# A graph layer's last stage: 8 of the 17 row tiles of a chunk split into float32r heads and tails before they are summed

## The chip, the cores and the metric

The kernel runs on one core of one Trainium2 chip. The metric is the device time of one execution in microseconds (us), lower is better. The times shown are those of three runs; the profile is of one profiled execution.

## What is computed

Two graph layers over 3125 nodes with 512 features and 50000 edges that are sorted by their destination. The first is attention over the edges, the second (the one that the change touches) a mean over neighbours with two linear maps:

```python
deg = jnp.maximum(segment_sum(ones, dst, 3125), 1.0)
h = jnp.maximum(_layernorm(x), 0.0)
x = x + attention_layer(h, ...)
h = jnp.maximum(_layernorm(x), 0.0)
agg = segment_sum(h[src], dst, 3125)
x = x + h @ W1.T + b1 + (agg / deg[:, None]) @ W2.T + b2
```

## The kernel before

The nodes are cut into 25 windows of 125, and the edges, sorted by destination, into chunks of up to 17 tiles of 128 edges (`CT = 17`). With this input there are 25 chunks, one for each window. The program sorts the edges on VectorE, runs the attention layer chunk by chunk, then the output product and the second normalisation (which stores the rows of h in the table `h2tab` in HBM), and then the last stage, which is what matters here. It takes the last 600 us or so of the span, and goes through the 25 chunks so:

- **GpSimd** (POOL) only gathers. For each tile `gather` (L494 on, the instruction is L501) issues one indirect DMA that reads 128 edge numbers from `idx` in SBUF and fetches 128 rows of 512 float32 out of `h2tab` into `arena` (seen as `rows`, two buffers of 17 tiles). The 17 tiles come in four parts, `PARTS = [(0, 3), (3, 4), (7, 5), (12, 5)]` (first tile, count), each with its own semaphore `rows_in` for rows that have landed and `rows_free` for rows that PE has finished with. The next chunk is gathered while this one is summed.
- **TensorE** (PE) adds the rows up by destination: for each tile one float32 product of the one-hot matrix `oh` (128 edges by 125 nodes, stationary) with the 128 by 512 rows (L907) into `aggp` in PSUM. In front stands a small product for the degrees (L903), behind it the product of the window's own rows with W1 (`product`, L758), the transposes of the mean `win_out` and of the next window's rows (`fin_cols`, L893), and the product with W2 (L758 again).
- **VectorE** (DVE) scales and adds the sum (L1453 to L1459), decodes the edge words of the chunk after next (L1230 to L1237), makes its one-hot matrix (`one_hot`, L1246, both inputs in SBUF) and reduces that for the degrees (L1401), and last adds the bias and the old x of this chunk (L1470, L1473).
- **ScalarE** (ACT) copies the transposed columns out of PSUM (L705), twice a chunk.
- **SyncE** (SP) loads edge words and the window's rows, and stores the output; it waits for `out_ready` of a chunk before it goes on to the loads of the next.

All order is by the program text and semaphores: no scheduler moves an instruction.

## Time and profile before

| what | value |
| --- | --- |
| median of 3 runs | 1963.72 us (1957.36 to 1965.88) |
| profiled execution: span from the first to the last instruction | 1960.7 us |
| profiled execution: its own time, taken as its span and the 3 us by which the median lies above it | 1963.7 us |
| TensorE busy | 1657.7 us (85%) |
| VectorE busy | 1368.6 us (70%) |
| GpSimd busy | 1143.8 us (58%) |
| ScalarE busy | 989.2 us (50%) |
| last stage, from its first gather (at 1363.0 us) to the end | 597.7 us |

The span is what the profile measures; the time of an execution holds a little more. For the execution with the profile no time of its own is given, so the table sets its span beside the median. Busy shares are averages over stages that differ: in the last stage ScalarE has almost nothing to do and TensorE nearly no pause. Busy time of TensorE is modelled from pipelined instructions, so the starts of its instructions are a better measure than their durations. A float32 product shows as two matmul instructions for each call.

### The profile page before, as it was taken

Reading aid. Unit: us, or ns where it says so; the run is one execution under the profiler, and the core shown is the slowest. Engines: PE = TensorE matmul, PEld = TensorE weight load, DVE = VectorE, ACT = ScalarE, POOL = GpSimd, SP = SyncE. Lnnn points to the kernel's source line nnn. Section 1 sums busy time; section 2 is a strip of 40 time slices with the busy share of each in tenths; the row PEclk is TensorE's granted clock in tenths of the full one; section 3 lists DMA queues with packets and bytes.
Section 4 is the critical chain, followed back from the end, with each engine's and each line's share of the span. In section 5 each row is a group of like instructions: output and inputs, shape, how many; then the busy total and the mean of one; then the engine's idle time right before and its main releaser. Section 6 shows DMA issues by size and latency. Waiting matters only on the chain.

```text
span 1960.7 us, 24166 instructions
## 1 busy us (share of the span) xinstructions
PE 1657.7 (85%) x5685; PEld 957.1 (49%) x5685; DVE 1368.6 (70%) x2637; ACT 989.2 (50%) x3754; POOL 1143.8 (58%) x1322
## 2 busy tenths in 40 slices
PE   3799842198989898988888888886999999999998
PEld 1343321066666665666666666443444444444443
DVE  8889888588989898989898987367344444444441
ACT  4453310659999999999999998242000000000000
POOL 2000000477888788878787882012777777777773
PEclk9899876599999999989998988898999999999999
DMA  8122101655666666656565652864777777777774
GB/s 185 53 66 79 62 30 42 192 162 152 181 170 178 172 177 171 177 165 183 164 184 159 189 155 56 198 155 122 211 216 216 217 220 212 222 218 215 209 215 141
DMA packets 133203, 318.09 MB, mean 162 GB/s; under 512 B 41908, under 2 KB 42158, under 8 KB 133044
## 3 DMA queue, kind: packets, MB, share of 16 engines
q0 software_dynamic: 70240, 229.93, 41.2%
q1 hardware_dynamic: 62804, 86.44, 15.9%
q8 instruction: 50, 0.82, 0.2%
q14 instruction: 109, 0.89, 0.1%
HBM read 280.43 MB, written 35.86 MB: 161 GB/s over the span
## 4 chain that ended last, share of the span: by engine, by line
PE 59%; DVE 22%; issue 11%; DMA 3%; ACT 2%; DVEq 1%; POOL 1%; SPq 0%; POOLq 0%; ACTq 0%
PE sums L907 19%; PE wide L758 17%; PE sums L810 11%; PE wide L838 8%; DVE arena L1061 3%; DVE arena L1060 3%; DVE nodes L1352 2%; DMA h2tab<-node 2%; DVE nodes L1298 1%; DVE nodes L1343 1%; DVE node L1239 1%; ACT node L705 1%; PE wide L753 1%; ACT arena L579 1%; PE wide L771 1%
## 5 line engine op out<-in xcount | busy, mean ns | idle before, releaser
L625 ACT ACTIVATE nodes<-arena,nodes 128x64 f32<-128x64 f32 x2840 | 682.7, 332 | 1.7 <-PE sums L810 1.5
L501 POOL DMA_INDIRECT arena<-ktab,idx x425 | 425.2, 1001 | 174.7 <-issue 115.4
L501 POOL DMA_INDIRECT arena<-h2tab,idx x425 | 444.1, 1045 | 135.7 <-issue 133.5
L810 PE MATMUL sums<-nodes,oh 128*125 128x260 f32 x1768 | 465.3, 406 | 44.1 <-DVE nodes L1298 44.1
L758 PE MATMUL wide<-w_sb,node 128*125 128x512 f32 x1000 | 468.4, 612 | 22.6 <-ACT node L564 14.2
L810 PEld LDWEIGHTS sums<-nodes,oh 128*125 128x125 f32 x1768 | 340.4, 197 | 120.3 <-DVE nodes L1298 55.5
L907 PE MATMUL sums<-arena,oh 128*125 128x512 f32 x850 | 374.8, 599 | 6.6 <-DMA arena<-h2tab,idx 6.6
L838 PE MATMUL wide<-q_win,node 125*128 125x512 bf16 x1275 | 311.5, 382 | 5.4 <-issue 5.4
L705 ACT ACTIVATE node<-wide 128x500 f32<-128x500 f32 x51 | 27.2, 585 | 569.5 <-PE wide L893 569.5
L758 PEld LDWEIGHTS wide<-w_sb,node 128*125 128x125 f32 x1000 | 184.8, 193 | 238.0 <-issue 208.5
L1343 DVE TENSOR_TENSOR nodes<-wide,arena 128x1024 f32<-128x1024 f32 (+1 forms) x225 | 258.5, 1158 | 12.8 <-PE wide L838 12.1
L907 PEld LDWEIGHTS sums<-arena,oh 128*125 128x125 f32 x850 | 158.8, 190 | 202.6 <-issue 191.7
L1352 DVE TENSOR_REDUCE nodes<-nodes 128x16 f32<-128x1024 f32 (+1 forms) x225 | 256.8, 1150 | 0.0
L525 POOL TENSOR_SCALAR oh<-iota,loc 128x125 f32<-128x125 f32 x425 | 246.8, 596 | 0.8
L1453 DVE SCALAR_TENSOR_TENSOR acc<-acc,first_chunk,sums 125x512 f32<-125x512 f32 x25 | 18.7, 747 | 303.4 <-PE sums L907 303.4
L838 PEld LDWEIGHTS wide<-q_win,node 125*128 125x128 bf16 x1275 | 177.9, 141 | 96.0 <-issue 9.8
L507 POOL DMA_DIRECT2D sorted_tab<-arena x2 | 1.2, 614 | 326.4 <-DVE arena L1107 326.4
L1061 DVE TENSOR_TENSOR arena<-arena 128x256 f32<-128x256 f32 x272 | 112.9, 415 | 0.0
L1060 DVE TENSOR_TENSOR arena<-arena 128x256 f32<-128x256 f32 x272 | 112.9, 415 | 0.0
L1401 DVE TENSOR_REDUCE junk<-oh 128x125 f32<-128x2125 f32 x25 | 104.1, 4166 | 0.9
L537 POOL DMA_DIRECT2D h2tab<-node x25 | 13.4, 535 | 153.0 <-ACT node L689 149.7
L1246 DVE TENSOR_TENSOR oh<-iota,loc 128x2125 f32<-128x2125 f32 x25 | 59.3, 2373 | 4.0 <-DVE loc L1237 4.0
(199 smaller groups left out, 1157.1 us busy)
## 6 DMA issues: line engine op xcount, KB each, us to landing
node<-node_tab SPq DMA_DIRECT2D x27, 531.2 KB
q_win<-qtab SPq DMA_DIRECT2D x26, 336.0 KB
arena<-ktab,idx POOLq DMA_INDIRECT x425, 5.3
arena<-h2tab,idx POOLq DMA_INDIRECT x425, 3.9
h2tab<-node POOLq DMA_DIRECT2D x25, 250.0 KB, 2.8
node<-h2tab SPq DMA_DIRECT2D x26, 224.0 KB
qtab<-q_win SPq DMA_DIRECT2D x17, 336.0 KB
nodes<-x SPq DMA_DIRECT2D x5, 1120.0 KB
```

The lines of the kernel that those rows point to most:

```text
L501: gp.indirect_dma_start(rows[:, b, t, :], None, tab, bass.IndirectOffsetOnAxis(ap=idx[:, b, t:t + 1], axis=0)).then_inc(s["rows_in"][b][PA ...
L525: last = gp.tensor_scalar(oh[:, b, t, :], iota[:, 0:WIN], loc[:, b, t + 1:t + 2], None, ALU.is_equal)
L625: last = act.activation(msgs[:, t, h // HH, h % HH * DH:(h % HH + 1) * DH], rows[:, 1 - b, t, h * DH:(h + 1) * DH], ACT.Copy, scale=den_in ...
L758: last = pe.matmul(out, ncol[:, b, c, :], w_sb[:, w, c, :], start=start and c == 0, stop=stop and c == KC - 1)
L810: last = pe.matmul(halves[:, u, :], oh[:, 1 - b, t, :], rhs[side][:, t, u, :], start=t == 0, stop=t == CT - 1)
L838: last = pe.matmul(wide[n % 2][:, (t - t0) * D:(t - t0 + 1) * D], ohT[:, b, :].rearrange("p (e t) -> p t e", t=CT)[:, t, :], q_win[:, b, p ...
L907: last = pe.matmul(aggp, oh[:, b, t, :], rows[:, b, t, :], start=t == 0, stop=t == CT - 1)
L1060: self.made(dve.tensor_tensor(new[:, :, 0, :], old[:, :, 0, :], old[:, :, 1, :], ALU.min))
L1061: self.made(dve.tensor_tensor(new[:, :, 1, :], old[:, :, 0, :], old[:, :, 1, :], ALU.max))
L1343: made.append(st.mark(dve.tensor_tensor(prod[:, n % 3, 0:k * D], wide[n % 2][:, 0:k * D], rows[:, b, t0:t0 + k, :].rearrange("p t d -> p ( ...
L1352: summed.append(st.mark(dve.tensor_reduce(sc[:, :, t0:t0 + k].rearrange("p h t -> p t h"), prod[:, (n - 1) % 3, 0:k * D].rearrange("p (t h ...
L1401: dve.tensor_reduce(oh_sum[:, b, :], oh[:, b, :, :].rearrange("p t n -> p n t"), AX.X, ALU.add).then_inc(ag["kept"], 1)
```

## The change

Eight of a chunk's 17 tiles, those of part 1 (tiles 3 to 6) and the first four of part 2 (tiles 7 to 10), are no longer multiplied as float32. ScalarE copies the rows of four tiles at once (128 by 2048) into a float32r tile `heads` (L723 of the new file), VectorE subtracts the head from the row in place, again four tiles at once (`make_tails`, L1478), and PE multiplies the same one-hot matrix with the head and then with the tail, both as float32r (L928, L929), into the same sum. The other nine tiles stay as they were (L931). The heads have one buffer, so ScalarE also waits until PE is through with the former chunk's part. The arrays get new names over the same memory (`late_rows` over `arena`, `late_oh` over `oh`, `heads` over `q_win`).

```diff
+        head_made, tail_made = sem("head_made"), sem("tail_made")
+        HEADED = [(3, 4, 1), (7, 4, 2)]
...
-            chunks(gp, count1, lambda g, b, i: gather(ag, h2tab, g, b))
+            chunks(gp, count1, lambda g, b, i: gather(ag, h2tab, late_rows[:, :, :, :].bitcast(F32), g, b))
...
+            def make_heads(g, b, i):
+                for n, (t0, k, part) in enumerate(HEADED):
+                    act.wait_ge(ag["rows_in"][b][part], (i + 1) * PARTS[part][1] * 16)
+                    act.wait_ge(ag["rows_free"][part], g + 2)
+                    act.activation(heads[:, n * 4:n * 4 + k, :], late_rows[:, b, t0:t0 + k, :].bitcast(F32), ACT.Copy).then_inc(head_made, 1)
             def fin(g, b, i):
+                make_heads(g, b, i)
                 fin_turned(1, g * 2 + 2, ag["out_free"])
                 fin_turned(0, g * 2 + 3, s5["row_free"])
...
-                        last = pe.matmul(aggp, oh[:, b, t, :], rows[:, b, t, :], start=t == 0, stop=t == CT - 1)
+                        for m, (first, _, _) in enumerate(HEADED):
+                            if t == first:
+                                pe.wait_ge(tail_made, g * len(HEADED) + m + 1)
+                        if t in HEAD_AT:
+                            pe.matmul(aggp, late_oh[:, b, t, :], heads[:, HEAD_AT[t], :], start=False, stop=False)
+                            last = pe.matmul(aggp, late_oh[:, b, t, :], late_rows[:, b, t, :], start=False, stop=False)
+                        else:
+                            last = pe.matmul(aggp, late_oh[:, b, t, :].bitcast(F32), late_rows[:, b, t, :].bitcast(F32), start=t == 0, stop=t == CT - 1)
...
+            def make_tails(g, b):
+                for n, (t0, k, _) in enumerate(HEADED):
+                    dve.wait_ge(head_made, g * len(HEADED) + n + 1)
+                    part_rows = late_rows[:, b, t0:t0 + k, :]
+                    dve.tensor_tensor(part_rows, part_rows.bitcast(F32), heads[:, n * 4:n * 4 + k, :].bitcast(F32), ALU.subtract).then_inc(tail_made, 1)
+            make_tails(0, 0)
...
                 given(dve, within(g + 2, count1), next_hot)
+                given(dve, within(g + 1, count1), lambda: make_tails(g + 1, 1 - b))
```

VectorE's order in the last stage, for the end of one chunk's turn and the start of the next, before (`oh` is the one-hot matrix, `node` holds the output rows, `acc` the sum):

```order
L1230 TENSOR_SCALAR idx<-pk 128x17 [waits ag_step,ag_pk_in0]
L1232 TENSOR_SCALAR keyi<-pk 128x17
L1233 COPY first_chunk<-par 128x1
L1237 TENSOR_SCALAR loc<-keyi,par 128x17 [waits ag_decode]
L1246 TENSOR_TENSOR oh<-iota,loc 128x2125 [waits ag_decode,ag_idx_ready]
L1401 TENSOR_REDUCE junk<-oh 128x125 [waits ag_oh_ready]
L1467 TENSOR_LOAD chunk_i
L1467 ISA x2
L1470 TENSOR_TENSOR node<-wide,junk 125x512 [waits fin_sum_ready,fin_out_free]
L1473 ISA [waits fin_step]
L1473 TENSOR_TENSOR node<-node,nodes 125x512
L1453 SCALAR_TENSOR_TENSOR acc<-acc,first_chunk,sums 125x512 [waits ag_acc_ready]
```

and now:

```order
L1254 TENSOR_SCALAR idx<-pk 128x17 [waits ag_step,ag_pk_in0]
L1256 TENSOR_SCALAR keyi<-pk 128x17
L1257 COPY first_chunk<-par 128x1
L1261 TENSOR_SCALAR loc<-keyi,par 128x17 [waits ag_decode]
L1270 TENSOR_TENSOR late_oh<-iota,loc 128x2125 [waits ag_decode,ag_idx_ready]
L1425 TENSOR_REDUCE junk<-late_oh 128x125 [waits ag_oh_ready]
L1478 TENSOR_TENSOR late_rows<-late_rows,heads 128x2048 [waits head_made] x2
L1500 TENSOR_LOAD chunk_i
L1500 ISA x2
L1503 TENSOR_TENSOR node<-wide,junk 125x512 [waits fin_sum_ready,fin_out_free]
L1506 ISA [waits fin_step]
L1506 TENSOR_TENSOR node<-node,nodes 125x512
```

Two subtractions, each with a wait for a head of the next chunk, stand between the one-hot work and the output rows of this chunk.

PE's order for one chunk, before (one row for a call; `sums` is the sum in PSUM, `junk` the summed one-hot matrix):

```order
L903 MATMUL sums<-ones,junk 125x1
L907 MATMUL sums<-arena,oh 125x512 x17
L758 MATMUL wide<-w_sb,node 125x512 x4
L893 MATMUL wide<-ident,win_out 128x125 x4
L893 MATMUL wide<-ident,node 128x125 x4
L758 MATMUL wide<-w_sb,node 125x512 x4
```

and now, the first and the last rows of the same piece:

```order
L920 MATMUL sums<-ones,junk 125x1
L931 MATMUL sums<-late_rows,late_oh 125x512 x3
L928 MATMUL sums<-heads,late_oh 125x512
L929 MATMUL sums<-late_rows,late_oh 125x512
L928 MATMUL sums<-heads,late_oh 125x512
...
L929 MATMUL sums<-late_rows,late_oh 125x512
L931 MATMUL sums<-late_rows,late_oh 125x512 x6
L775 MATMUL wide<-w_sb,node 125x512 x4
```

The pair of head and tail stands there eight times, where eight float32 products stood. GpSimd's order is the same as before.

## Rows read from the trace of the kernel before

**Rows 1.** Groups of instructions, 1398 to 1961 us: busy, mean ns; idle before, releaser

```profile
L501 POOL DMA_INDIRECT arena<-h2tab,idx x399 | 418.8, 1050 | 121.5 <-issue 119.7 <-DVE idx L1230 1.8
L907 PE MATMUL sums<-arena,oh 128*125 128x512 f32 x816 | 356.1, 595 | 0.0
L705 ACT ACTIVATE node<-wide 128x500 f32<-128x500 f32 x48 | 25.6, 585 | 529.6 <-PE wide L893 529.6
L1453 DVE SCALAR_TENSOR_TENSOR acc<-acc,first_chunk,sums 125x512 f32<-125x512 f32 x24 | 17.9, 747 | 280.3 <-PE sums L907 280.3
```

**Rows 2.** Timeline of PE, one chunk and the next one's start: start us, us

```profile
1538.87 14.84 PE L907 MATMUL sums<-arena,oh 128*125 128x512 f32 x34
1553.54 3.60 PE L758 MATMUL wide<-w_sb,node 128*125 128x512 f32 x8
...
1558.33 3.70 PE L758 MATMUL wide<-w_sb,node 128*125 128x512 f32 x8 [0.34 <-ACT node L705]
1561.87 0.28 PE L903 MATMUL sums<-ones,junk 128*125 128x1 f32 x2
1562.00 14.84 PE L907 MATMUL sums<-arena,oh 128*125 128x512 f32 x34
```

**Rows 3.** Timeline of POOL, 1556 to 1581 us

```profile
1556.07 0.95 POOL L501 DMA_INDIRECT arena<-h2tab,idx  x1 [0.30 <-issue]
1557.32 3.06 POOL L501 DMA_INDIRECT arena<-h2tab,idx  x1 [0.30 <-issue]
1560.69 0.94 POOL L501 DMA_INDIRECT arena<-h2tab,idx  x1 [0.30 <-issue]
...
1580.68 3.06 POOL L501 DMA_INDIRECT arena<-h2tab,idx  x1 [0.30 <-issue]
```

**Rows 4.** Timeline of DVE, same stretch

```profile
1557.19 2.37 DVE L1246 TENSOR_TENSOR oh<-iota,loc 128x2125 f32<-128x2125 f32 x1 [0.18 <-DVE loc L1237]
1559.60 4.17 DVE L1401 TENSOR_REDUCE junk<-oh 128x125 f32<-128x2125 f32 x1
```

**Rows 5.** Timeline of all engines at the stage's start

```profile
1368.09 0.69 DVE L1447 TENSOR_TENSOR junk<-junk 125x512 f32<-125x512 f32 x1
1368.21 1.38 POOL L501 DMA_INDIRECT arena<-h2tab,idx  x1 [0.30 <-issue]
1369.90 0.94 POOL L501 DMA_INDIRECT arena<-h2tab,idx  x1 [0.31 <-issue]
```

**Rows 6.** Line L501's gathers of h2tab: ns min/median/max; time to landing

```profile
L501 POOL DMA_INDIRECT arena<-h2tab,idx x425: 942/946/3067, 1363.0 to 1935.3; - x142
...
DMA to landing us min/median/max: 3.4/3.9/6.2
```

**Rows 7.** Timeline of the attention stage, POOL and DVE

```profile
619.01 1.49 POOL L501 DMA_INDIRECT arena<-ktab,idx  x1 [0.30 <-issue]
...
618.73 1.83 DVE L1298 TENSOR_TENSOR nodes<-arena,nodes 128x768 f32<-128x768 f32 x2 [0.32 <-DVE rden L1316]
```

**Rows 8.** Groups of ACT, shapes apart: busy, mean ns

```profile
L625 ACT ACTIVATE nodes<-arena,nodes 128x64 f32<-128x64 f32 x2840 | 682.7, 332 | 1.7 <-PE sums L810 1.5
...
L594 ACT ACTIVATE q_win<-node 125x512 bf16<-125x512 f32 x17 | 10.6, 622 | 0.2 <-DVE node L1134 0.2
```

**Rows 9.** Timeline of PE: a float32r product (L771) and bfloat16 ones (L838)

```profile
154.91 0.49 PE L771 MATMUL wide<-bias_row,ones_row 33*125 33x512 f32 x1
155.33 3.70 PE L758 MATMUL wide<-w_sb,node 128*125 128x512 f32 x8
...
654.93 1.46 PE L838 MATMUL wide<-q_win,node 125*128 125x512 bf16 x6
656.23 1.04 PE L810 MATMUL sums<-nodes,oh 128*125 128x260 f32 x4
```

**Rows 10.** Last chunk: start of PE's sums, last gather, in two views of the timeline

```profile
1932.13 14.84 PE L907 MATMUL sums<-arena,oh 128*125 128x512 f32 x34
...
1935.27 0.94 POOL L501 DMA_INDIRECT arena<-h2tab,idx  x1 [0.30 <-issue]
```

**Rows 11.** Windows: PE, PEld, DVE, ACT, POOL busy (x), granted clock, DMA share, GB/s

```profile
1365.00:1400.00 35.00, 27.97 (x66) 12.86 (x66) 10.70 (x15) 1.65 (x3) 26.77 (x28) 0.82 0.74 209
...
1376.00:1381.20 5.20, 2.70 (x7) 0.91 (x5) 0.00 (x0) 0.00 (x0) 3.84 (x5) 1.00 0.71 212
1381.20:1385.00 3.80, 3.78 (x5) 1.66 (x6) 0.00 (x0) 0.00 (x0) 2.89 (x4) 0.55 0.71 199
```

More of the change, by code:

```diff
@@ L64, in build @@
         chunk_tab = [dram(f"chunk_tab{j}", [GTAB, 2]) for j in range(2)]
-        arena = sb("arena", [128, 2 * CT * D])
+        with ExitStack() as under_rows:
+            arena = under_rows.enter_context(nc.sbuf_tensor("arena", [128, 2 * CT * D], F32))
+        late_rows = sb("late_rows", [128, 2, CT, D], F32R)
         rows = arena[:, 0:2 * CT * D].rearrange("p (b t d) -> p b t d", b=2, t=CT)
@@ L94, in build @@
             ones_row = under_oh.enter_context(nc.sbuf_tensor("ones_row", [BR, 128], F32R))
-        oh = sb("oh", [128, 2, CT, WIN])
+        with ExitStack() as under_late_oh:
+            oh = under_late_oh.enter_context(nc.sbuf_tensor("oh", [128, 2, CT, WIN], F32))
+        late_oh = sb("late_oh", [128, 2, CT, WIN], F32R)
         junk = sb("junk", [128, 2, HALF])
@@ L112, in build @@
         oh_sum = junk[:, 0, 0:2 * WIN].rearrange("p (b n) -> p b n", b=2)
-        q_win = sb("q_win", [WIN, 2, SPLIT, D], BF16)
+        HEADED = [(3, 4, 1), (7, 4, 2)]
+        with ExitStack() as under_heads:
+            q_win = under_heads.enter_context(nc.sbuf_tensor("q_win", [WIN, 2, SPLIT, D], BF16))
+        heads = sb("heads", [128, sum(k for _, k, _ in HEADED), D], F32R)
         q_parts = q_win
@@ L232, in build @@
         at, ag = chunk_sems("at"), chunk_sems("ag")
+        head_made, tail_made = sem("head_made"), sem("tail_made")
+        HEAD_AT = {t0 + k: n * 4 + k for n, (t0, tiles, _) in enumerate(HEADED) for k in range(tiles)}
         q_in = [sem("q_in0"), sem("q_in1")]
@@ L494, in _, with gather @@
             gp.sem_inc(consts, 1)
-            def gather(s, tab, g, b, first=0, end=CT):
+            def gather(s, tab, into, g, b, first=0, end=CT):
                 hold(gp, "pool", s["idx_ready"], g + 1)
@@ L500, in gather @@
                         hold(gp, "pool", s["rows_free"][PART[t]], g + 1)
-                    gp.indirect_dma_start(rows[:, b, t, :], None, tab,
+                    gp.indirect_dma_start(into[:, b, t, :], None, tab,
                                           bass.IndirectOffsetOnAxis(ap=idx[:, b, t:t + 1], axis=0)).then_inc(s["rows_in"][b][PART[t]], 16)
@@ L516, in _ @@
             count = chunk_count(gp, 0)
-            gather(at, ktab, 0, 0)
+            gather(at, ktab, rows, 0, 0)
             def one_hot(g, b):
@@ L528, in attend @@
             def attend(g, b, i):
-                given(gp, within(g + 1, count), lambda: gather(at, ktab, g + 1, 1 - b, 0, PARTS[2][0]))
+                given(gp, within(g + 1, count), lambda: gather(at, ktab, rows, g + 1, 1 - b, 0, PARTS[2][0]))
                 one_hot(g, b)
-                given(gp, within(g + 1, count), lambda: gather(at, ktab, g + 1, 1 - b, PARTS[2][0], CT))
+                given(gp, within(g + 1, count), lambda: gather(at, ktab, rows, g + 1, 1 - b, PARTS[2][0], CT))
             chunks(gp, count, attend)
@@ L1245, in one_hot @@
             def one_hot(s, g, b):
[L1246 removed]
+                dve.tensor_tensor(late_oh[:, b, :, :], iota[:, 0:WIN].unsqueeze(1).to_broadcast([128, CT, WIN]),
                                   loc[:, b, 1:CT + 1].unsqueeze(2).to_broadcast([128, CT, WIN]), ALU.is_equal).then_inc(s["oh_ready"], 1)
```

3 lines of the change are left out of this document (1 added, 2 removed).

## The prediction

> **What bounds the kernel now.** The change touches the last stage alone, so I read that stretch. The grouped view of it [rows 1] shows PE's sums as the costliest group with no idle time before them, ACT waiting 529.6 us and DVE 280.3 us for PE: by the shares PE is the bound. The timeline of PE [rows 2] says the same: a chunk's sums start at 1538.87 and the next chunk's at 1562.00, a period of 23.13 us, in which the 34 matmul instructions of the 17 tiles take 1553.54 − 1538.87 = 14.67 us, 0.432 us each, 0.863 us a tile.
>
> But POOL is as close. Its timeline [rows 3] shows a gather every 1.25 us, with 0.30 us of issue between them and no wait for a free buffer: [rows 1] put 119.7 of the 121.5 us of its idle time down to issue, 0.30 us for each of 399 gathers. A chunk needs 17 × 1.25 = 21.25 us of that. And one gather in each chunk takes 3.06 us where the others take 0.95 [rows 3]; DVE's timeline [rows 4] shows what stands there: the one-hot compare L1246, a TENSOR_TENSOR with both inputs in SBUF, runs from 1557.19 to 1559.56, and the gather that began at 1557.32 ends at 1560.38, 0.82 us after it. The next gather, beside the reduction L1401 (one input), takes its usual 0.94 us. The same shows without broadcast inputs: L1447, 512 elements from SBUF and SBUF, ends at 1368.78, and the gather that began 0.12 us after it did ends at 1369.59, 0.81 us after that, 0.43 us longer than an undisturbed one [rows 5]; and in the attention stage a gather is stretched to 1.49 us by L1298, which ends its first half about 619.65 us, and goes through before the second half [rows 7]. So a gather reads something 0.13 us after its start; if DVE then holds a two-input operation from SBUF, the gather stops until that operation's end.
>
> How long? A read comes each 1.25 us, so an operation of L us that begins at any phase holds one gather for L − 1.25 to L, L − 0.625 in the mean. For L1246 (2.37) that is 1.75 us; the rows give (1050 − 946) ns × 399 gathers [rows 1, 6] over 22 compares in that stretch = 1.89 us. POOL's own period is then 21.25 + 1.89 = 23.14 us: it has nothing to spare against PE's 23.13. What there is between them is one lead: PE comes to the last five tiles of the last chunk at 1932.13 + 24 × 0.432 = 1942.5 us, and their last rows, gathered at 1935.27, land about 3.9 us later, at 1939.2 [rows 6, 10]. That is 3.3 us of slack in the whole stage.
>
> **What PE gains.** Each of 8 tiles changes 0.863 us of float32 for two float32r passes. The nearest rows are far apart [rows 9]: a float32r product of 512 columns that stands alone takes 155.33 − 154.91 = 0.42 us to the next instruction, and bfloat16 passes of 512 columns in a row take (656.23 − 654.93) / 6 = 0.217 us. Two passes are so 0.43 to 0.84 us, and PE's chunk shrinks by 8 × 0.43 = 3.4 us at best, by 0.2 us at worst. I take 0.217, since the passes stand in rows of 16; for the time it makes little difference, since POOL cannot follow.
>
> The Trainium skill (FP8 and Floating Point Precision, TensorE Precision Notes) says that a true float32 product is four passes; two single passes would then be half the work, the 3.4 us, and by a sum on PE alone the kernel would be some 80 us faster. The lone pass of [rows 9] does not show that half, since it costs as much as one of the two instructions of a float32 product.
>
> **What ACT adds.** Two copies of 128 × 2048 a chunk. Between 64 elements (332 ns) and 512 (622 ns) [rows 8] an element costs 0.65 ns, so 0.33 + 1984 × 0.65 ns = 1.6 us each; at 1 ns an element it would be 2.2. I take 1.9. ACT is busy 25.6 of 563 us here [rows 1], so this is hidden, as long as rows come before heads do: it adds 1.9 us from landing to a usable head. Its two waits hold only its own L705 copies of the next chunk behind them.
>
> **What DVE adds.** Two subtractions of 2048 elements a chunk, both inputs in SBUF. From 512 elements at 0.69 us [rows 5] to 2125 at 2.37 [rows 4] an element costs 1.04 ns, so 2.29 us each, 4.6 us a chunk. DVE waits 280.3 / 24 = 11.7 us a chunk for PE now [rows 1], so its own time fits. Queued behind them are the output rows of the chunk (L1470, L1473) and with them SP, which holds the loads after the store. From the heads of part 2 to the next sum there remain over 5 us (part 3 needs five more gathers, 6.25 us), and what SP loads is needed only after that sum; I cost this at nothing. If the cover went, the output rows would be late by the 4.6 us at most once a chunk, and PE's transposes with them.
>
> **What POOL pays.** The subtractions are the kind of operation that stops a gather. Each is tied to rows that POOL itself delivers, so each falls into the next gathers and not between stages: a stall of 1.04 to 2.29 us, in the mean 2.29 − 0.625 = 1.67. I take the mean, as L1246's own mean came out near it. Two a chunk, 25 chunks: 50 × 1.67 = 83.5 us. The period becomes 21.25 + 1.75 + 3.3 = 26.3 us against PE's 19.7 to 23.1: the stage turns from PE to POOL.
>
> **The sum.** 3.3 us of the 83.5 go into the slack; the last chunk ends as before, with five float32 tiles and the two products behind its last rows. 83.5 − 3.3 = 80.2 us. The profiled execution has a span of 1960.7 and, at some 3 us more, a time of 1963.7, which is also the median. 1963.7 + 80.2 = 2043.9, so 2044 us, 4.1% slower. Bounds: with 1.04 us for each stall 52 − 3.3 = 49 us (2013), with 2.29 us 114.5 − 3.3 = 111 us (2075). L1246's own stall, now that POOL sets the phase, may move between 1.12 and 2.37 us for its 23 compares, −15 to +14 us from today. All at an end together is unlikely; half of that beside the bounds gives 2005 to 2081.
>
> The Trainium skill (SBUF — State Buffer, Who interferes with whom) has both answers: a DVE instruction with two SBUF inputs contends with a GpSimd instruction that reads SBUF, and in the same list it is said, as an inference, that descriptor generation needs only the write side, and that tensor_tensor was not seen to stall a DMA. By the first the time is the 2044 above, by the second that of the first rival below. The rows of this trace agree with the first.
>
> **Rivals.**
> - *The subtractions do not stop the gathers, or fall between their reads.* For it: L1473, also with two SBUF inputs but short, mostly falls between two reads, and nothing here shows a float32r output. Against: three lines of [rows 3 to 5, 7] stop gathers, and 2.29 us is longer than the 1.25 between reads, so none can fall between. Then PE's chunk shrinks to 19.7 us, and POOL's 21.25 + 1.12 to 1.89 us is the bound: 0 to 0.77 us a chunk and the slack, 1942 to 1964 us, with L1246 at its mean 21.25 + 1.75 = 23.0, about 1958. It decides if a subtraction holds a gather under 0.1 us. No change is likelier in it than a gain.
> - *PE stays the bound and grows.* If float32r passes take 0.42 us each, PE needs 23 us a chunk and has waits for two tails in it. After a pause of 2.51 us before 1381.22 the granted clock falls from 1.00 to 0.55 in the next 3.8 us, and over the stage's start, with such pauses, it is 0.82 [rows 11]. PE's 23.1 us at 0.82 is 28.2 us, 1.9 over POOL's 26.3: 25 × 1.9 = 47 us more, 2091 us. Against it: the pauses vanish once PE is the bound, and the clock comes back.
> - *The wait moves to the queue behind the subtractions*: output rows, SP's loads, transposes. With 4.6 us late each chunk it would be worth up to 115 us, but it is in parallel to the stalls and needs the 5 us of cover gone. It is inside the upper part of the range.
>
> **How the numbers follow.** The stalls by the subtractions, with POOL as the bound: 0.81, of which the queue case is 0.04. PE as the bound, slower still: 0.08. No stalls: 0.11, of which 0.09 within 0.5% (10 us, about what a measurement of this kernel tells from no change) and 0.02 a gain over that. So faster 0.02, same 0.09, slower 0.89. The range 2005 to 2081 takes in the first case but for its ends.
>
> **What would show it.** Right: POOL's period about 26.3 us, three stretched gathers in each chunk instead of one, each ending 0.82 us after a TENSOR_TENSOR of DVE (L1270, L1478, L1478); the mean gather near 1.24 us; idle time on PE before L931 or L928, put down to the gather; no wait of POOL for a buffer. The subtraction at 2.29 us, the head near 1.9 us, the two passes starting 0.22 us (or 0.42) apart. Wrong: gathers of 0.95 us beside L1478; a period of 23 us or less; POOL waiting for `rows_free` or for the edge words; PE without pauses.

## The result, and the profile after

| what | before | after |
| --- | --- | --- |
| median (lowest to highest), 4 runs each | 1964.2 us (1957.36 to 1965.88) | 2037.24 us (2033.14 to 2041.13) |
| profiled execution: span, own time | 1960.7 us, not given | 2032.5 us, 2034.36 us |
| GpSimd busy | 1143.8 us | 1223.9 us |
| last stage, first gather to the end | 597.7 us | 675.8 us (from 1356.7) |

The change makes the kernel slower: ratio 1.0388, 95% interval 1.0368 to 1.0409 (the two medians of the table alone give 1.037). The forecast was 2044 us.

The costliest groups of the whole execution, from the page of the changed kernel (busy us, mean ns of one; idle us before it and its main releaser):

```profile
L510 POOL DMA_INDIRECT late_rows<-h2tab,idx x425 | 523.4, 1232 | 135.5 <-issue 134.9
...
L931 PE MATMUL sums<-late_rows,late_oh 128*125 128x512 f32 x450 | 238.4, 672 | 60.7 <-DMA late_rows<-h2tab,idx 60.6
...
L1485 DVE SCALAR_TENSOR_TENSOR acc<-acc,first_chunk,sums 125x512 f32<-125x512 f32 x25 | 18.7, 748 | 239.2 <-PE sums L931 239.2
...
L723 ACT ACTIVATE heads<-late_rows 128x2048 fp32r<-128x2048 f32 x50 | 95.6, 1911 | 104.8 <-DMA late_rows<-h2tab,idx 104.7
L1478 DVE TENSOR_TENSOR late_rows<-late_rows,heads 128x2048 fp32r<-128x2048 f32 x50 | 114.2, 2287 | 36.3 <-ACT heads L723 36.2
L928 PE MATMUL sums<-heads,late_oh 128*125 128x512 f32 x200 | 85.0, 425 | 53.6 <-DVE late_rows L1478 53.5
```

A reader of [rows 1] sees the roles changed. PE's sums, without idle time before, now wait 60.7 us for rows to land and 53.6 us for tails. POOL still has next to no idle time but issue, the pause from one gather to the next (134.9 of 135.5 us, 0.32 us a gather), so it waits for nobody; what has grown is the gather itself, 1232 ns in the mean. The same gathers took 444.1 us before, so POOL's busy time rose by 523.4 − 444.1 = 79.3 us; the median of the whole kernel rose by 73.0.

One chunk on POOL in the changed kernel, from the timeline (start us, duration us):

```profile
1604.59 3.06 POOL L510 DMA_INDIRECT late_rows<-h2tab,idx  x1 [0.30 <-issue]
1607.95 0.94 POOL L510 DMA_INDIRECT late_rows<-h2tab,idx  x1 [0.30 <-issue]
...
1611.70 2.34 POOL L510 DMA_INDIRECT late_rows<-h2tab,idx  x1 [0.30 <-issue]
1614.35 2.20 POOL L510 DMA_INDIRECT late_rows<-h2tab,idx  x1 [0.30 <-issue]
1616.85 1.23 POOL L510 DMA_INDIRECT late_rows<-h2tab,idx  x1 [0.30 <-issue]
```

DVE in the same stretch of the same trace:

```profile
1604.45 2.37 DVE L1270 TENSOR_TENSOR late_oh<-iota,loc 128x2125 fp32r<-128x2125 f32 x1 [0.17 <-DVE loc L1261]
1606.86 4.17 DVE L1425 TENSOR_REDUCE junk<-late_oh 128x125 f32<-128x2125 f32 x1
1610.95 2.28 DVE L1478 TENSOR_TENSOR late_rows<-late_rows,heads 128x2048 fp32r<-128x2048 f32 x1
1613.43 2.29 DVE L1478 TENSOR_TENSOR late_rows<-late_rows,heads 128x2048 fp32r<-128x2048 f32 x1 [0.20 <-ACT heads L723]
1615.64 0.68 DVE L1503 TENSOR_TENSOR node<-wide,junk 125x512 f32<-125x512 f32 x1
1616.57 0.69 DVE L1506 TENSOR_TENSOR node<-node,nodes 125x512 f32<-125x512 f32 x1 [0.24 <-DVE node L1503]
```

Lay the two over each other. L1270 ends at 1606.82, the first long gather at 1607.65. The subtractions end at 1613.23 and 1615.72, their gathers at 1614.04 and 1616.55; L1506 ends at 1617.26, its gather at 1618.08. All four stand 0.81 to 0.83 us apart, as in [rows 3 to 5]. Beside the reduction L1425, 4.17 us with one input, the gathers take 0.94 to 0.95 us. Summed over the stage by the operation beside which they ended, the stretched gathers cost, above 0.945 us each: L1270 45.3 us (24 chunks), L1478 68.1 us (50 subtractions, 1.36 each), L1506 6.9 us (24). In the kernel before it was 41.5 us for the compare L1246 and next to nothing beside the output rows.

PE in the same chunk of the changed kernel:

```profile
1609.47 2.82 PE L931 MATMUL sums<-late_rows,late_oh 128*125 128x512 f32 x6
1613.37 0.47 PE L928 MATMUL sums<-heads,late_oh 128*125 128x512 f32 x1 [1.08 <-DVE late_rows L1478]
1613.68 0.40 PE L929 MATMUL sums<-late_rows,late_oh 128*125 128x512 f32 x1
1613.91 0.40 PE L928 MATMUL sums<-heads,late_oh 128*125 128x512 f32 x1
...
1615.87 0.47 PE L928 MATMUL sums<-heads,late_oh 128*125 128x512 f32 x1 [0.39 <-DVE late_rows L1478]
...
1617.79 1.02 PE L931 MATMUL sums<-late_rows,late_oh 128*125 128x512 f32 x2
1621.11 4.56 PE L931 MATMUL sums<-late_rows,late_oh 128*125 128x512 f32 x10 [2.30 <-DMA late_rows<-h2tab,idx]
```

A float32r pass follows the next after 0.23 us, so PE did get its relief. It spends it waiting three times: for each group of tails, and 2.30 us for the rows of part 3. The chain of waits of the changed kernel says it in one line:

```profile
PE 31%; POOL 22%; DVE 22%; issue 19%; DMA 3%; ACT 2%; DVEq 1%; SPq 0%; POOLq 0%; ACTq 0%
POOL late_rows L510 22%; PE sums L827 10%; PE wide L775 9%; PE wide L855 8%; DVE arena L1084 2%; DVE arena L1085 2%; DVE nodes L1376 2%; DMA h2tab<-node 2%; DVE nodes L1322 1%; DVE nodes L1367 1%; DVE node L1263 1%; PE sums L931 1%; PE wide L770 1%; ACT arena L588 1%; PE wide L788 1%
```

22% of 2032.5 us is 447 us of gathers, in a stage of 676; L931 has 1%.

### The profile page after: what moved, and what is told of

It is laid out like the page before. It is cut to its first block, busy times and chain, and to the rows that moved or that the text cites. A ratio compares the mean times of both kernels' runs of the same rounds, so it can differ in the third digit from the quotient of the medians.

```text
span 2032.5 us, 24367 instructions
## 1 busy us (share of the span) xinstructions
PE 1621.0 (80%) x5685; PEld 958.9 (47%) x5685; DVE 1479.6 (73%) x2687; ACT 1082.9 (53%) x3804; POOL 1223.9 (60%) x1322
## 4 chain that ended last, share of the span: by engine, by line
PE 31%; POOL 22%; DVE 22%; issue 19%; DMA 3%; ACT 2%; DVEq 1%; SPq 0%; POOLq 0%; ACTq 0%
POOL late_rows L510 22%; PE sums L827 10%; PE wide L775 9%; PE wide L855 8%; DVE arena L1084 2%; DVE arena L1085 2%; DVE nodes L1376 2%; DMA h2tab<-node 2%; DVE nodes L1322 1%; DVE nodes L1367 1%; DVE node L1263 1%; PE sums L931 1%; PE wide L770 1%; ACT arena L588 1%; PE wide L788 1%
## 5 line engine op out<-in xcount | busy, mean ns | idle before, releaser
L510 POOL DMA_INDIRECT late_rows<-h2tab,idx x425 | 523.4, 1232 | 135.5 <-issue 134.9
L827 PE MATMUL sums<-nodes,oh 128*125 128x260 f32 x1768 | 457.4, 401 | 44.8 <-DVE nodes L1322 44.8
L827 PEld LDWEIGHTS sums<-nodes,oh 128*125 128x125 f32 x1768 | 335.7, 195 | 118.9 <-DVE nodes L1322 56.5
L931 PE MATMUL sums<-late_rows,late_oh 128*125 128x512 f32 x450 | 238.4, 672 | 60.7 <-DMA late_rows<-h2tab,idx 60.6
L931 PEld LDWEIGHTS sums<-late_rows,late_oh 128*125 128x125 f32 x450 | 91.0, 212 | 173.6 <-issue 90.5
L723 ACT ACTIVATE heads<-late_rows 128x2048 fp32r<-128x2048 f32 x50 | 95.6, 1911 | 104.8 <-DMA late_rows<-h2tab,idx 104.7
L1478 DVE TENSOR_TENSOR late_rows<-late_rows,heads 128x2048 fp32r<-128x2048 f32 x50 | 114.2, 2287 | 36.3 <-ACT heads L723 36.2
L928 PE MATMUL sums<-heads,late_oh 128*125 128x512 f32 x200 | 85.0, 425 | 53.6 <-DVE late_rows L1478 53.5
```

Of the source, the lines that this page charges most:

```text
L510: gp.indirect_dma_start(into[:, b, t, :], None, tab, bass.IndirectOffsetOnAxis(ap=idx[:, b, t:t + 1], axis=0)).then_inc(s["rows_in"][b][PA ...
L827: last = pe.matmul(halves[:, u, :], oh[:, 1 - b, t, :], rhs[side][:, t, u, :], start=t == 0, stop=t == CT - 1)
L931: last = pe.matmul(aggp, late_oh[:, b, t, :].bitcast(F32), late_rows[:, b, t, :].bitcast(F32), start=t == 0, stop=t == CT - 1)
L1478: dve.tensor_tensor(part_rows, part_rows.bitcast(F32), heads[:, n * 4:n * 4 + k, :].bitcast(F32), ALU.subtract).then_inc(tail_made, 1)
```

## Experiments

The theory under test: DVE operations with two SBUF inputs hold POOL's gathers, and that alone turns the stage from PE to POOL. Rivals: the subtractions cost by something else (waits for heads, the queue on DVE, PE's clock), or the gathers were never what bound.

### First set

Four kernels. The chip on which they ran is a slower one for this program: the kernel before took 2247.04 us there (2227 to 2255), so their expectations, which are in times of the first chip, can be judged by ratio and rows alone. The edits: `e1_extra_subs` is the kernel before, with two subtractions on DVE in memory that nothing else uses in this stage (it is cleared once before the stage's first sum):

```diff
+        extra = sb("extra", [128, 8, D])
...
+                for n in range(2):
+                    dve.wait_ge(extra_done, g * 2 + n + 1)
+                    dve.tensor_tensor(extra[:, 0:4, :], extra[:, 4:8, :], extra[:, 4:8, :], ALU.subtract).then_inc(extra_done, 1)
```

> The kernel before with two subtractions of 128 x 2048 float32 added to each chunk on VectorE, both inputs in SBUF, on arrays of zeros that nobody waits for; TensorE's sums and ScalarE are as before, and what is computed is the same. Theory (a two-input operation from SBUF stops GpSimd's gathers): POOL's period goes from 23.1 to 25.6 to 26.4 us, three stretched gathers in each chunk, 2022 to 2042 us. Rival 1 (the time is lost by PE's waits for heads and tails, or by the split product): nothing of that is here, 1964 us. Rival 2 (VectorE's own time): its 11.7 us of waiting in a chunk hold the 4.6 us, 1964 us.

`e2_one_input` is the changed kernel with a reduction (one input) in place of the subtraction; PE multiplies the head twice, since there are no tails, so the result leaves the tails out:

```diff
-                            last = pe.matmul(aggp, late_oh[:, b, t, :], late_rows[:, b, t, :], start=False, stop=False)
+                            last = pe.matmul(aggp, late_oh[:, b, t, :], heads[:, HEAD_AT[t], :], start=False, stop=False)
...
-                    dve.tensor_tensor(part_rows, part_rows.bitcast(F32), heads[:, n * 4:n * 4 + k, :].bitcast(F32), ALU.subtract).then_inc(tail_made, 1)
+                    dve.tensor_reduce(small[:, n, 0:1], part_rows.bitcast(F32).rearrange("p t d -> p (t d)"), AX.X, ALU.add).then_inc(tail_made, 1)
```

> The changed kernel, but each subtraction is replaced by a sum over the same 2048 elements of the rows (one input, 2.3 to 2.5 us), and PE multiplies the head twice; the tails are left out of the result. All waits, the copies and the number of products are the same. Theory: the gathers beside it stay at 0.95 us, one stretched gather a chunk, POOL's period 22.4 to 23.2 us, 1947 to 1966 us. Rival (waits for heads and tails): same order and same waits, so 2030 to 2040 us.

`e3_pieces` cuts each subtraction into four of one tile:

```diff
-                    dve.tensor_tensor(part_rows, part_rows.bitcast(F32), heads[:, n * 4:n * 4 + k, :].bitcast(F32), ALU.subtract).then_inc(tail_made, 1)
+                    for t in range(k):
+                        one = part_rows[:, t, :]
+                        last = dve.tensor_tensor(one, one.bitcast(F32), heads[:, n * 4 + t, :].bitcast(F32), ALU.subtract)
+                    last.then_inc(tail_made, 1)
```

> The changed kernel with each subtraction cut into four of 128 x 512 (0.69 us each, one behind the other); the same result. Theory (a gather goes through in the gap between two operations): two reads fall into the 2.5 us of a group and each waits for the end of its piece alone, 0.35 us in the mean, so some 0.7 us for a group instead of 1.25 to 1.4: period 24.2 to 24.8 us, 1985 to 2008 us. Rival (VectorE's whole time with two inputs counts): 2037 us or a little more.

`e4_head_in_psum` lets ACT copy each tile's head on into a spare half of a PSUM bank, so that the subtraction has one SBUF and one PSUM input (the diff is shown below, with its second run):

> The changed kernel, but ScalarE also copies each tile's head into one of two free PSUM banks, and VectorE subtracts that (one input in SBUF, one in PSUM, 4 pieces of 512); the same result. Theory: no subtraction holds a gather, one stretched gather a chunk (the one-hot compare), period 22.4 to 23.2 us, 1947 to 1966 us. Rival (latency of heads and tails): ScalarE's copies make the way from landing to tail 2 to 3 us longer, so 2037 us or more.

Measured: e1 2176.55 us, ratio 0.9701 (0.9648 to 0.9753); e2 2231.95 us, 0.9936 (0.988 to 0.9991); e3 2185.67 us, 0.9751 (0.9693 to 0.9809); e4 2248.18 us, 1.0008 (0.9939 to 1.0077). None of the expected times was met, and on this chip adding two useless subtractions even went with a shorter time. These ratios price nothing for the first chip. What they do show is in the rows. First DVE's timeline in e2, one-input reductions, then POOL's beside them:

```profile
1701.68 4.49 DVE L1478 TENSOR_REDUCE small<-late_rows 128x1 f32<-128x2048 f32 x2
```

```profile
1701.17 0.94 POOL L510 DMA_INDIRECT late_rows<-h2tab,idx  x1 [0.30 <-issue]
1702.42 0.95 POOL L510 DMA_INDIRECT late_rows<-h2tab,idx  x1 [0.30 <-issue]
1703.67 0.94 POOL L510 DMA_INDIRECT late_rows<-h2tab,idx  x1 [0.30 <-issue]
```

The same rows read and PE served in the same places, yet no gather beside a reduction is held, in any chunk. The mean gather was 1060 ns in e2 against 1192 in e1; the compare and the last addition of the output rows still hold theirs. In e3 the eight short subtractions of a chunk (4.99 us in one run) mostly stretched one gather, to 1.07 to 1.39 us, and let the others through at 0.94 to 0.95, mean 1093 ns. But of the 22 such runs that have gathers beside them two held one gather to their very end, as in these rows of e3, first DVE's, then POOL's:

```profile
1954.39 4.91 DVE L1480 TENSOR_TENSOR late_rows<-late_rows,heads 128x512 fp32r<-128x512 f32 x8
```

```profile
1955.13 4.99 POOL L510 DMA_INDIRECT late_rows<-h2tab,idx  x1 [0.30 <-issue]
```

The two runs took 4.91 and 4.92 us, the others 4.97 to 5.06. What decides whether a read gets in between two short operations is not shown.

Why the time there did not follow, the DVE timeline of e3 shows in part:

```profile
1726.38 0.75 DVE L1488 SCALAR_TENSOR_TENSOR acc<-acc,first_chunk,sums 125x512 f32<-125x512 f32 x1 [12.07 <-remote]
```

DVE's wait for the chunk's sum ends here by something that the trace names on no engine of the core. Most of the 12.07 us is the usual wait for PE; what is new is the end of it. PE went on from this sum to its next product at 1721.84, and DVE began 4.5 us after that. In the kernels before and after on the first chip it begins 0.20 us after, and so it does in e1 in 23 of 25 chunks. In e2 it is 5.0 to 7.9 us in 23 of 25 chunks, in e4 3.5 to 5.2 us. So e1 runs its last stage at 26.3 us a chunk, near the 25.8 of the same kernel on the faster chip of the second set, while e2 and e4 take 28.5 and 29.0. The other part of the loss lies ahead of the stage: it begins at 1492.8 us in e1 and at 1360.7 in the same kernel of the second set. What the delay is I did not find out, and no trace shows the kernel before on such a chip, so why it took longer there than e1 is not shown.

### Second set: the price on the first chip's pace

The same two kernels again, on a chip where the kernel before took 1961.24 us (1958.14 to 1965.89).

> The same kernel as e1_extra_subs once more, because in the chip job of e1 to e4 the kernel before itself took 2247 us where it had taken 1964, so that gathers were bound by something else there. If the kernel before takes some 1964 us here. Theory (a two-input operation from SBUF stops a gather): POOL's period 25.6 to 26.4 us, three stretched gathers a chunk, 2022 to 2042 us. Rivals (waits for heads and tails; VectorE's own time): 1964 us. If the kernel before is again near 2247 us, the gathers beside the added subtractions are still stretched by the theory, and the time tells nothing.

Measured: 2022.77 us (2021.19 to 2023.45), ratio 1.0304 (1.0277 to 1.033). Neither heads, nor tails, nor waits for them, nor float32r were in it: the kernel before and two subtractions without purpose. POOL in f1, one chunk:

```profile
1598.94 3.06 POOL L504 DMA_INDIRECT arena<-h2tab,idx  x1 [0.30 <-issue]
...
1606.06 2.33 POOL L504 DMA_INDIRECT arena<-h2tab,idx  x1 [0.30 <-issue]
1608.70 2.02 POOL L504 DMA_INDIRECT arena<-h2tab,idx  x1 [0.30 <-issue]
1611.03 1.23 POOL L504 DMA_INDIRECT arena<-h2tab,idx  x1 [0.30 <-issue]
```

DVE in f1:

```profile
1605.30 4.61 DVE L1473 TENSOR_TENSOR extra<-extra 128x2048 f32<-128x2048 f32 x2
1609.82 0.68 DVE L1478 TENSOR_TENSOR node<-wide,junk 125x512 f32<-125x512 f32 x1
1610.75 0.69 DVE L1481 TENSOR_TENSOR node<-node,nodes 125x512 f32<-125x512 f32 x1 [0.24 <-DVE node L1478]
```

It is the pattern of the changed kernel, 3.06, 2.33, 2.02, 1.23, at a mean gather of 1198 ns against 1232. 59.4 us of stalls fall to the 50 subtractions (1.19 each) and the time rose by 61.5. The last addition of the output rows, L1481, holds a gather here too (1.23 us, 6.8 us above 0.945 in the stage). Of the 73 us that the change costs, the operand reads alone so make about 60.

`f2_head_in_psum`:

```diff
-        head_made, tail_made = sem("head_made"), sem("tail_made")
+        head_made, copied, bank_free = sem("head_made"), sem("copied"), sem("bank_free")
...
+                    act.wait_ge(head_made, g * len(HEADED) + n + 1)
+                    for t in range(k):
+                        act.wait_ge(bank_free, g * 8 + n * 4 + t + 1)
+                        act.activation(wide[t % 2][:, D:2 * D], heads[:, n * 4 + t, :].bitcast(F32), ACT.Copy).then_inc(copied, 1)
...
-                                pe.wait_ge(tail_made, g * len(HEADED) + m + 1)
+                                pe.wait_ge(bank_free, 2 + g * 8 + m * 4 + 4)
...
-                    dve.tensor_tensor(part_rows, part_rows.bitcast(F32), heads[:, n * 4:n * 4 + k, :].bitcast(F32), ALU.subtract).then_inc(tail_made, 1)
+                    for t in range(k):
+                        dve.wait_ge(copied, g * 8 + n * 4 + t + 1)
+                        one = part_rows[:, t, :]
+                        dve.tensor_tensor(one, one.bitcast(F32), wide[t % 2][:, D:2 * D], ALU.subtract).then_inc(bank_free, 1)
```

> The same kernel as e4_head_in_psum once more, for the same reason: the subtraction takes the head from PSUM. If the kernel before takes some 1964 us here. Theory: no gather is stretched beside a subtraction, one a chunk beside the one-hot compare, POOL's period 22.4 to 23.2 us, 1947 to 1966 us. Rival (latency of heads and tails, or the number of operations on VectorE and ScalarE): 2037 us or more.

Measured: 2034.63 us (2029.66 to 2039.78), ratio 1.0371 (1.0335 to 1.0406): the time that the theory gave was missed by 69 us at its upper end, though its mechanism is in the rows. The timeline of f2, first DVE, then POOL:

```profile
1604.35 2.38 DVE L1275 TENSOR_TENSOR late_oh<-iota,loc 128x2125 fp32r<-128x2125 f32 x1 [0.17 <-DVE loc L1266]
1606.76 4.19 DVE L1430 TENSOR_REDUCE junk<-late_oh 128x125 f32<-128x2125 f32 x1
1610.88 2.62 DVE L1486 TENSOR_TENSOR late_rows<-late_rows,wide 128x512 fp32r<-128x512 f32 x4
1615.35 2.64 DVE L1486 TENSOR_TENSOR late_rows<-late_rows,wide 128x512 fp32r<-128x512 f32 x4 [1.85 <-ACT wide L727]
1618.01 0.69 DVE L1511 TENSOR_TENSOR node<-wide,junk 125x512 f32<-125x512 f32 x1
1618.95 0.69 DVE L1514 TENSOR_TENSOR node<-node,nodes 125x512 f32<-125x512 f32 x1 [0.24 <-DVE node L1511]
```

```profile
1604.68 2.87 POOL L510 DMA_INDIRECT late_rows<-h2tab,idx  x1 [3.14 <-DVE idx L1259]
...
1611.60 0.94 POOL L510 DMA_INDIRECT late_rows<-h2tab,idx  x1 [0.30 <-issue]
1612.85 0.95 POOL L510 DMA_INDIRECT late_rows<-h2tab,idx  x1 [0.30 <-issue]
...
1616.60 0.95 POOL L510 DMA_INDIRECT late_rows<-h2tab,idx  x1 [0.30 <-issue]
...
1619.09 1.37 POOL L510 DMA_INDIRECT late_rows<-h2tab,idx  x1 [0.30 <-issue]
```

Beside the subtractions from PSUM every gather takes 0.94 to 0.95 us, in every chunk; what still holds one is the compare L1275 and the last addition L1514 (0.42 us in 21 chunks), both SBUF and SBUF. But POOL now waits about 3 us a chunk for edge numbers. As I read it, DVE's order makes a ring: compare, reduction, two groups of subtractions with ACT's copies between them, then the output rows (1618 to 1619.6), then SP's store and, some 5 us behind it, the next edge words. SP's queue in the timeline of f2:

```profile
1619.86 0.91 SPq L464 DMA_DIRECT2D out<-node  x2
1624.89 0.38 SPq L375 DMA_DIRECT2D pk<-sorted_tab  x1
1625.32 0.43 SPq L376 DMA_DIRECT2D par<-chunk_tab  x1
```

From these DVE decodes `idx`, which POOL wants (next gather at 1630.91). From one sum to the next f2 takes 26.0 us in the mean, the changed kernel 26.2: another bound lay just beneath POOL's. That it is this ring is read from the rows and not shown: in the same trace PE waits 73.3 us for tails between 1398 and 1961 us, more than the 54.0 us that POOL waits for edge numbers, and a sum that comes late by its tails makes the decoding late too.

### Third set: the order, and the compare

The kernel before took 1961.1 us here (1955.57 to 1965.31, 19 runs). `g1_out_first_psum` is f2 with both groups of subtractions behind the output rows:

```diff
-                given(dve, within(g + 1, count1), lambda: make_tails(g + 1, 1 - b))
...
                 dve.tensor_tensor(nout[:, b, 0, :], nout[:, b, 1, :], x_sb[:, bass.ds(w, 1), :].rearrange("p a d -> p (a d)"), ALU.add).then_inc(s5["out_ready"], 1)
+                given(dve, within(g + 1, count1), lambda: make_tails(g + 1, 1 - b))
```

> f2_head_in_psum with one more edit: VectorE adds the chunk's output rows before the subtractions for the next chunk and not behind them. Theory (f2 was bound by a ring: output rows, SP's store and its wait of 5 us, SP's loads of edge words, decoding, compare 2.4, reduction 4.2, subtractions 2 x 2.6, output rows, 26.2 us in all; the subtractions' 5.3 us and ScalarE's waits leave the ring now): no gather is stretched beside a subtraction, the ring is short enough, and the period falls to 22.4 to 23.6 us, 1945 to 1975 us. Rival (the latency from rows over head, copy and subtraction to PE is what binds f2): the period stays at 25 to 26 us, 2010 to 2035 us.

Measured: 2065.3 us (2057.39 to 2067.42), ratio 1.0522 (1.0497 to 1.0546); both theories missed, on the slow side. The output rows are early, but the subtractions are not: they stand behind compare, reduction and output rows, and PE waits 98.9 us for them between 1398 and 1961 us. From a sum to the next there is, as I read it, one chain, decode, compare, reduction, output rows, two groups of subtractions in turn with ACT's copies, the last products. PE's pauses also cost it clock: the granted clock is 0.89 between 1500 and 1900 us, where the kernel before had 1.00. That moving the output rows ahead did not help speaks against the ring through SP as the only bound of f2.

`g2_reorder` is the changed kernel, its subtractions unaltered from SBUF, with the first group before the output rows, the second behind them, and the one-hot work of the chunk after next last:

```diff
+                given(dve, within(g + 2, count1), lambda: decode(ag, g + 2, b, i + 1))
+                given(dve, within(g + 1, count1), lambda: make_tails(g + 1, 1 - b, (0,)))
...
+                given(dve, within(g + 1, count1), lambda: make_tails(g + 1, 1 - b, (1,)))
+                given(dve, within(g + 2, count1), lambda: sum_hot(g + 2, b))
```

> The changed kernel, with its subtractions in SBUF, and VectorE's order in a chunk turned to: decode, first subtraction, output rows, second subtraction, compare, reduction. Theory (the changed kernel is bound by the stretched gathers of POOL, three of them in each chunk wherever they stand): 25.4 to 26.6 us a chunk, 2018 to 2042 us. Rival (the changed kernel is bound by the ring over the output rows and SP, and the stretched gathers only fill the time): the ring is 6 us shorter, 1950 to 1990 us.

Measured: 2020.42 us (2014.55 to 2023.06), ratio 1.0295 (1.0277 to 1.0314). With a far shorter ring the changed kernel gains 17 us and no more: it is POOL, not the ring, that holds it. Its gathers wait 2.1 us in all for edge numbers, and their mean is 1190 ns. Even the 17 us are POOL's: its gathers are busy 505.9 us for 523.4. The compare, now behind the second subtraction, holds them for 24.2 us in the stage where it held them for 45.3, while the subtractions cost 71.7 us for 68.1.

`g3_all` puts both together, and the compare too reads its iota from PSUM (the column for the degrees moves to another bank):

```diff
+        iota_p = tiny[:, 64:64 + WIN]
+        degp = turn[1][0:WIN, 500:501]
...
-                dve.tensor_tensor(late_oh[:, b, :, :], iota[:, 0:WIN].unsqueeze(1).to_broadcast([128, CT, WIN]),
+                dve.tensor_tensor(late_oh[:, b, :, :], iota_p.unsqueeze(1).to_broadcast([128, CT, WIN]),
```

> Both: heads for the subtraction in PSUM, VectorE's order of g2, and the compare's iota in PSUM too (the degree column moves to another bank for that). Theory: no two-input operation from SBUF but the last addition (0.69 us) is left, POOL's period is 21.25 us and up to 0.4, PE's about 20 to 22.5 with its waits: 21.4 to 22.6 us a chunk, 1920 to 1952 us, faster than both kernels. Rival (something else binds at 23 us): 1955 to 1966 us.

Measured: 1968.24 us (1960.74 to 1970.59, 10 runs), ratio 1.003 (1.0018 to 1.0042). The groups of g3 from 1398 to 1961 us:

```profile
L511 POOL DMA_INDIRECT late_rows<-h2tab,idx x396 | 375.5, 948 | 158.0 <-issue 115.1 <-DVE idx L1260 43.0
...
L1491 DVE TENSOR_TENSOR late_rows<-late_rows,wide 128x512 fp32r<-128x512 f32 x192 | 123.3, 683 | 116.4 <-ACT wide L728 113.0
...
L934 PE MATMUL sums<-heads,late_oh 128*125 128x512 f32 x192 | 95.4, 497 | 45.3 <-DVE late_rows L1491 45.3
```

948 ns: next to no gather is held any more, and 69 us of the loss is gone (2037.24 to 1968.24). It fell short of the 1920 to 1952 expected, because what took over is delay and not work: DVE waits 113.0 us for ACT's copies, PE 45.3 us for the last of the subtractions, POOL 43.0 us for edge numbers. No engine is the bound by its work alone. What I did not price is the clock: over 1398 to 1961 us PE was granted 0.95 where the kernel before had 1.00, and a float32 instruction of its sums took 627 ns in the mean for 595. PE's busy time (509.1 us) and its waits for subtractions and for ScalarE's copies of transposed rows (45.3 and 8.4 us) fill the 563 us: the stage is as long as PE's work at that clock and these waits.

`g4_hot_in_psum` is the kernel before with only the compare's iota in PSUM:

> The kernel before, with only the compare's iota in PSUM. Theory (PE bounds the kernel before at 23.13 us, and POOL only just keeps up): no gather is stretched any more, the mean gather falls from 1.05 to 0.95 us, and the time stays: 1958 to 1966 us. Rival (POOL's stretched gather is what sets the period): 21.4 us a chunk, 1925 us.

Measured: 1957.99 us (1955.48 to 1961.53, 10 runs), ratio 0.999 (0.998 to 1.0001). The timeline of g4 at a compare, where [rows 3] have a gather of 3.06 us, first POOL, then DVE:

```profile
1598.85 0.94 POOL L502 DMA_INDIRECT arena<-h2tab,idx  x1 [1.68 <-DVE idx L1231]
```

```profile
1598.53 2.37 DVE L1247 TENSOR_TENSOR oh<-sums,loc 128x2125 f32<-128x2125 f32 x1 [0.18 <-DVE loc L1238]
```

The compare takes its 2.37 us as before and holds nothing: the mean gather falls from 1045 to 957 ns, 37 us of POOL's busy time, and the time does not move. From one sum to the next it is 23.13 us in both. So PE bound the kernel before, and POOL did not.

### Fourth set: half the dose

What shortens g3's chain is one group instead of two. `h1_one_group4` is g3 with tiles 7 to 10 alone, the output rows written before the subtractions and the one-hot work behind them, `h2_one_group5` with tiles 7 to 11:

```diff
-        HEADED = [(3, 4, 1), (7, 4, 2)]
+        HEADED = [(7, 4, 2)]
```

> Only tiles 7 to 10 are split (one head, one group of four subtractions a chunk, PE relief 4 x (0.864 - 0.47) = 1.6 us); the compare reads its iota from PSUM and the head is copied into PSUM before it is subtracted, so that no VectorE operation over 0.7 us has two SBUF inputs; output rows are written before the subtractions and the reduction of the next one-hot matrix after them. Theory (the change paid for its operand reads and, with those gone, for the chain of two heads and two subtractions between one chunk's sum and the next): that chain is now one subtraction shorter and ends over 1 us before PE reaches tile 7, so PE's 23.07 - 1.6 + 0.1 = 21.6 us is the period, with POOL's 21.25 us just below: 1964 - 25 x 1.5 = 1927, range 1915 to 1945, gathers 0.95 us in the mean. Rival (what binds the version with both groups is not that chain but the loads of edge words behind the stored output rows, or the clock): the period stays at 23 us or more, 1955 to 1975, with POOL waiting for idx.

> The same with the whole of part 2 split (tiles 7 to 11, head of 128x2560, five subtractions, PE relief 2.0 us). PE would need 21.2 us a chunk, POOL 21.25, so POOL becomes the bound with no room: theory 1915 to 1940, no more than 8 us from the version with four tiles in either direction. If the chain through head and subtractions still binds, the fifth tile lengthens it by 1.1 us a chunk (0.5 for the head, 0.65 for the subtraction) and the time is 10 to 25 us above that of four tiles.

Measured, again where the kernel before is slow (2231.94 us, 2214.88 to 2260.06): h1 2190.22 us, ratio 0.9819 (0.977 to 0.9869); h2 2193.9 us, 0.9829 (0.9774 to 0.9883). The mean gather is 947 and 957 ns, and again DVE's wait for the sum ends by something unnamed, in h1 4.7 to 5.4 us after PE went on to its next product, in 23 of 25 chunks (the row is of an execution of h1 that took 2219.18 us):

```profile
1825.31 0.75 DVE L1496 SCALAR_TENSOR_TENSOR acc<-acc,first_chunk,sums 125x512 f32<-125x512 f32 x1 [7.17 <-remote]
```

That the fifth tile costs no 10 us was right (3.7 us between the medians), but so small a difference is inside the scatter of either there. Both ratios are below 1, but e1, with nothing but useless subtractions, had 0.9701 on a chip of that pace, so they are no evidence that half the dose wins. Whether it does on the first chip stays open, and the expected 1915 to 1945 us are untested. On the chips where the kernel before takes some 1961 us no version beats it by more than the measurement tells: g4, the best, has 0.999 (0.998 to 1.0001).

## Why the prediction was right

**What bounds before.** As read: PE, with POOL right beneath. Shown by g4 and f1: 37 us less on POOL change nothing, 65 us more (509.3 for 444.1) cost 61.5.

**PE's gain.** 8 tiles by (0.864 − 0.466) = 3.2 us, against 3.4; a float32r pass in a row takes 0.233 us, near the end of the bounds that was taken (0.217), and not the 0.42 us of the lone product of [rows 9]. By the rule of the Trainium skill (FP8 and Floating Point Precision, TensorE Precision Notes), four passes for a float32 product and so half the work for two, a headed tile is 0.43 us, as an estimate. The trace comes near that, with 2 × 0.233 = 0.47 us.

**ACT and DVE.** The head 1.911 us for 1.9, the subtraction 2.287 for 2.29.

**POOL's price.** This is the step that carried the forecast and it held; f1, e2 and f2 show it cause by cause. Its size was off in three terms that nearly cancel (−15.4, +6.9 and +3.8 us, with 2.3 us of slack not given back), and that they do is luck. The stall for each subtraction was put at 1.67 us and was 1.36: 68.1 us in place of 83.5. The mean over a random phase was the wrong mean, because the phase isn't random. The first subtraction starts right behind the reduction, 4.13 us after the compare's end, where POOL takes up its even pace again: reads come at each 1.25 us from there, the fourth at 5.0, so 4.13 + 2.29 − 5.0 = 1.42 us, measured 1.40 in the chunk shown and 1.38 to 1.44 in 22 others. The second follows 0.20 us behind the first, so one gather slips in between and the next is held 2.29 + 0.20 − 1.25 = 1.24 us, measured 1.26; where it waits longer for its head it holds up to 1.55. What was not predicted: L1506, the last addition of the output rows, 0.69 us, two SBUF inputs, now holds a gather in every chunk (0.29 us each, 6.9 in all), since that phase too is fixed. "Three stretched gathers in each chunk" are four. And L1270 costs 45.3 us for 41.5, inside the −15 to +14 us given.

**The slack at the end.** 3.3 us were to be given back, and 1.0 us was: from the last gather's start to the end 24.4 us in place of 25.4. The last rows came 4.5 us after their gather's start instead of 3.9, and the last ten instructions, behind a wait of 2.53 us, at a granted clock of 0.75 where the ten us before 2010 had 1.00, took 5.81 us (2012.57 to 2018.38) instead of 4.3.

**The sum.** The stage grew by 78.1 us against 80.2. Between the medians it is 73.0: in the profiled execution the stage began 6.3 us earlier (1356.7 for 1363.0), in a part of the program that the change doesn't touch. In f1 and g2 it began at 1360.7 and 1361.4; no run shows the cause, and it may be the scatter of single executions. The 3 us that I set between a span and its time were 1.9.

**Which of the two rules held.** All the long holds fall to operations with two SBUF inputs. Of the two answers of the Trainium skill (SBUF — State Buffer, Who interferes with whom) the first, two SBUF inputs against a POOL instruction that reads SBUF, so gave the time. The inference that the Trainium skill sets beside it, that descriptor generation needs only the write side and so is not touched by tensor_tensor, does not hold here for an indirect gather whose numbers lie in SBUF: 0.95 us became up to 3.06.

**The rivals.** No stall: false in every chunk. PE as the bound: false, PE waits for rows and tails, and the granted clock over 1398 to 2032 us was 0.95, not the 0.82 of its start. The queue behind the subtractions, put inside the range's upper part: it did not decide, as g2 shows, but it is near. f2 takes 26.0 us from sum to sum without a stall by the subtractions, 0.2 below the 26.2 of the changed kernel. I had costed this at nothing because SP's loads seemed early enough; they were so only as long as POOL was later still. Had I forecast f2's kernel by the steps of the prediction, I would have missed by some 70 us, as f2's expectation did. f2's chain also holds ScalarE's copies, so how much room the changed kernel itself had is not shown; the prediction worked out no such margin, and that there was one is in part luck.

## What to carry to other kernels

Before giving a busy stretch of a kernel more DVE work to relieve PE, ask who is second: here POOL needed 23.14 us a chunk by the prediction's working against PE's 23.13, so the relief had nowhere to go and the side effect counted in full. Price a DVE operation by where its inputs lie: two from SBUF stop an indirect gather beside it for up to the operation's length (0.95 us became up to 3.06 beside a compare of 2.37), one from PSUM and one from SBUF, or a reduction with one alone, cost it nothing (0.94 to 0.95 us); a cheap copy or constant in PSUM buys that off, if the extra step doesn't lengthen the chain from one chunk to the next. And where one engine sets the pace, the phases are fixed, so an average over phases is not what is paid, and short operations can pay in every round.

## What was not expected of the hardware

- The subtractions of a chunk as eight 512-element operations (e3) mostly held one gather, to at most 1.39 us, where the same work in two pieces held two, to some 2.3. It is mostly the length of the single operation that counts, but not surely: in two of 22 chunks one gather was held for the whole run, 4.99 us.
- An operation with one SBUF tensor can hold a gather too, if briefly: beside L1491 of the changed kernel (`win_out` out of `acc` and a column of factors, 0.48 us for 512 elements) seven gathers took 0.97 to 1.16 us, and ended 0.80 to 0.83 us after it like the others. It makes 0.7 us in the stage.
- float32r passes in a row stand 0.233 us apart, the first after a wait 0.31 (1613.37 to 1613.68), and one alone 0.42 [rows 9]. A float32 product of 512 columns (0.864 us) split into two float32r passes so pays in a run (0.47 us); two passes as far apart as the lone one (0.84 us) would gain next to nothing.
- Waits of a few us in each chunk go with a lower granted clock. Over 1500 to 1900 us it was 1.00 in the kernel before and in g4, 0.93 in g2, 0.89 in g1.
- One program took 1961 and 2232 to 2247 us on different chips. On the slow ones DVE began 3.5 to 7.9 us late behind PE's sum in nearly every chunk of e2, e4, h1 and h2, by 2.2 us or more in ten of e3's 25 and in hardly any of e1's, by something that the trace does not name, so a ratio found there says little for another chip. A small gain should be confirmed on the chip on which it was found.
